# Local attention on one core: where x1 is kept, two buffers for the score image, softmax sums on 32x32 blocks, and five value products a head on GpSimd

## What is computed

```python
x = x + _L0_conv_ref(_gn(x), ...)   # window attention, 16 heads of 16, windows of 49 pixels
x = x + _L1_conv_ref(_gn(x), w_out, b_out)

def _L1_conv_ref(x, w_out, b_out):          # KSIZE 5, PAD 2, NHEADS 8
    patches = extract_patches(x)            # the 25 shifts of each pixel, zeros outside
    p = patches.reshape(N, NHEADS, hdim, K2, H, W)
    q = x.reshape(N, NHEADS, hdim, 1, H, W)
    scores = (p * q).sum(axis=2, keepdims=True)
    att = jax.nn.softmax(scores, axis=3)
    out = (p * att).sum(axis=3).reshape(N, D, H, W)
    out = jnp.einsum('ndhw,od->nohw', out, w_out) + b_out[None, :, None, None]
    return out
```

## Time and profile before

| | |
|---|---|
| median of 3 runs | 1961.32 us (1961.11 to 1963.88) |
| the profiled execution | 1962.19 us |
| its span, first to last instruction | 1960.4 us |
| VectorE / TensorE / GpSimd / ScalarE busy | 83% / 79% / 59% / 53% of the span |
| 16 DMA engines, hardware queue | 20.5% |
| granted TensorE clock | 0.897 |

### The profile page before, as it was taken

The page is one execution under the profiler, slowest core; times in us unless marked ns, Lnnn a source line. Parts: engine busy times, 40 slices in busy tenths (PEclk is TensorE's granted clock), DMA queues, the critical chain, the costliest instruction groups (busy, mean ns, idle before and its releaser), DMA issues.

```text
span 1960.4 us, 53519 instructions
## 1 busy us (share of the span) xinstructions
PE 1557.5 (79%) x21545; PEld 789.1 (40%) x21545; DVE 1627.2 (83%) x2105; ACT 1044.7 (53%) x1927; POOL 1162.3 (59%) x843
## 2 busy tenths in 40 slices
PE   5889999999999999244986949859598595994935
PEld 3667777777777777100221212212122121221413
DVE  5987777777777777479999999899999999999724
ACT  3566677766777666234455554554645545444200
POOL 4434544444545445004869969698796987964800
PEclk9999999999999999675997969969799697996968
DMA  6000000000000000422014140141401404005069
GB/s 266 1 1 33 4 29 33 0 33 0 33 0 33 0 41 14 115 52 52 2 45 112 29 114 16 43 113 28 111 20 43 113 25 113 21 14 223 23 231 401
DMA packets 46596, 126.42 MB, mean 64 GB/s; under 512 B 12644, under 2 KB 24932, under 8 KB 41316
## 3 DMA queue, kind: packets, MB, share of 16 engines
q1 hardware_dynamic: 46436, 124.04, 20.5%
HBM read 79.04 MB, written 38.54 MB: 60 GB/s over the span
## 4 chain that ended last, share of the span: by engine, by line
PE 51%; DVE 28%; issue 10%; ACT 5%; SPq 2%; DMA 1%; DVEq 1%; POOLq 0%; POOL 0%; ACTq 0%
PE PS L1380 11%; PE PS L1267 8%; DVE PS L1140 7%; PE PS L1357 7%; DVE arena L1159 6%; PE PS L1255 6%; PE PS L1343 5%; PE PS L1221 4%; PE PS L1246 3%; DVE consts L1101 3%; DVE arena L1148 2%; PE PS L1400 2%; DVE arena L1053 2%; DVE arena L1134 2%; PE PS L1225 2%
## 5 line engine op out<-in xcount | busy, mean ns | idle before, releaser
L777 POOL TENSOR_TENSOR arena<-arena 128x1856 f32<-128x1856 f32 (+8 forms) x182 | 670.8, 3726 | 237.5 <-ACT arena L911 188.5
L1159 DVE TENSOR_TENSOR arena<-arena,PS 128x1568 f32<-128x1568 f32 x382 | 658.9, 1781 | 26.8 <-PE PS L1380 25.2
L1343 PE MATMUL PS<-arena,consts 128*32 128x285 f32 (+10 forms) x2176 | 252.6, 540 | 197.8 <-POOL arena L777 128.0
L1380 PE MATMUL PS<-arena,consts 32*32 32x392 f32 x12800 | 385.3, 511 | 22.8 <-DVE arena L1159 22.3
L735 POOL TENSOR_TENSOR arena<-arena,consts 128x196 f32<-128x196 f32 x512 | 294.2, 609 | 161.5 <-ACT arena L825 157.0
L953 ACT ACTIVATE PS<-arena 128x392 f32<-128x392 f32 x382 | 190.9, 501 | 344.2 <-DVE arena L1159 342.3
L1267 PE MATMUL PS<-arena 128*128 128x96 f32 x2048 | 265.7, 273 | 3.1 <-ACT arena L838 1.6
L1267 PEld LDWEIGHTS PS<-arena 128*128 128x128 f32 x2048 | 249.9, 192 | 5.3 <-issue 3.5
L1357 PE MATMUL PS<-arena,consts 128*128 128x392 f32 x400 | 193.2, 578 | 52.2 <-DVE arena L1148 52.2
L742 POOL TENSOR_TENSOR arena<-arena 128x392 f32 (+1 forms) x64 | 78.6, 1228 | 255.2 <-DVE arena L1080 255.2
L1343 PEld LDWEIGHTS PS<-arena,consts 128*32 128x32 f32 x2176 | 50.3, 115 | 396.0 <-issue 182.2
(11 more groups left out here) (97 smaller groups left out, 1663.1 us busy)
## 6 DMA issues: line engine op xcount, KB each, us to landing
arena<-x_dram SPq DMA_DIRECT2D x32, 616.0 KB, 7.5
arena<-x_dram SPq DMA_DIRECT2D x240, 77.0 KB, 2.0
arena<-in_x_dram SPq DMA_DIRECT2D x8, 1568.0 KB, 14.7
x_dram<-arena SPq DMA_DIRECT2D x8, 1568.0 KB, 5.2
attn_dram<-arena SPq DMA_DIRECT2D x256, 49.0 KB, 1.9
arena<-x_dram SPq DMA_DIRECT2D x8, 1568.0 KB, 17.6
arena<-attn_dram SPq DMA_DIRECT2D x8, 1568.0 KB, 17.6
out_dram<-arena SPq DMA_DIRECT2D x8, 1568.0 KB, 24.7
```

Of the source, the lines that this page charges most:

```text
L777: nc.gpsimd.tensor_tensor(tile, x_part, by, ALU.mult).then_inc(pool_tile, 1)
L1159: nc.vector.tensor_tensor(by_channel(v_tiles[n % V_RING]), shifted_values(half, k), over_channels(PS[:, 2 + n % W_BANKS, 0:PIX]), ALU.mult ...
L1343: mm = nc.tensor.matmul(PS[g * GROUP:(g + 1) * GROUP, 0, 0:(hi - lo) * cols], fold, tile[:, (g * rows + lo) * cols:(g * rows + hi) * cols] ...
L1380: mm = nc.tensor.matmul(PS[dst, 4 + i, 0:PIX], ident[src, src], tile[src, c * PIX:(c + 1) * PIX], start=done == 0, stop=done == NK - 1)
```

## The change

1. x1 is stored twice: as before (`x1_dram`, unpadded, for the end) and in `x1_wide_dram`, rows of 60 with two zero columns at either side and two zero rows around each channel's images. 12 DMAs of zeros fill it at the start (a new tile `zeros`, 2250 elements a partition); then each unit's 7 rows a partition are stored by one DMA of its own (`widen_x1`, 64 DMAs of 128 x 7 pieces of 56 elements).
2. Strips are loaded with their padding straight into the image (one DMA for a group, source 4 x 32 x 660 elements, destination 128 x 660) and normalised in place; `raw` is gone, and so are the GpSimd memsets of the padding. The score image of x has two buffers for each half, so head j+2 is loaded when head j's products are done. Of heads 0 and 1 the strips of groups 0 and 2 are loaded before the last three pairs are finished.
3. Score products cover only the 56 columns (1568, 1792 or 2016 elements), begin with dy = 2, and have their operands exchanged at dx = -1. No segments any more; the mirror is copied without its outermost columns, which `clear_borders` zeroes with four small copies a head.
4. The sums over the shifts use four 32x32 blocks instead of one 128x128 matrix.
5. In heads 0 to 6 GpSimd takes five value products (16 and 18 of half 0; 17, 21 and 22 of half 1); operands exchanged at dx = -1 there too. In head 7 it takes 17 of 50. The reciprocal comes nine value products before a head's end.
6. A half is stored in 4 DMAs (source 128 x 392, destination 4 x 32 x 392) instead of 16.

```diff
-HALF_PLANE = [(0, 0), (0, 1), (0, 2)] + [(dy, dx) for dy in (1, 2) for dx in range(-2, 3)]
+HALF_PLANE = [(dy, dx) for dy in (2, 1) for dx in range(-2, 3)] + [(0, 2), (0, 1), (0, 0)]
...
-RECIPROCAL_AT = 47
+RECIPROCAL_AT = 9
...
-SHARE_AT = [9, 17]
-POOL_SHARE = [[range(0), range(0)]] * (LH - 1) + [[range(16, NK), range(16, NK)]]
+SHARE_AT = [[9, 13], [18, 21, 24]]
+POOL_SHARE = [[(16, 18), (17, 21, 22)]] * (LH - 1) + [[range(18, NK), range(15, NK)]]
...
-        raw = [room(CH * RAW) for _ in range(2)]
-        xs_halves = room(2 * GROUPS * HALO).rearrange("p (a g h w) -> p a g h w", a=2, g=GROUPS, h=HR)
+        xs_halves = [room(GROUPS * HALO).rearrange("p (g h w) -> p g h w", g=GROUPS, h=HR) for _ in range(4)]
...
+            r0, rows = R - dy, GR + dy
+            X = xs_halves[s_buf(j, a)]
+            tile = ring[RING_AT[step] % S_RING][:, 0:GROUPS * rows * W]
+            here, there = X[:, :, r0:r0 + rows, R:R + W], X[:, :, R:R + rows, R + dx:R + dx + W]
+            if dx == -1:
+                here, there = there, here
...
+            def widen_x1(u):
+                sp.wait_ge(added, u + 1)
+                bp, row = u // NI, u % NI
+                src = xs[:, bp, :].rearrange("p (a i w) -> p a i w", i=NI, w=W)[:, :, row]
+                dst = x1_wide[:, bp].rearrange("p (a i) w -> p a i w", i=NI)[:, :, row, R:R + W]
+                sp.dma_start(dst, src).then_inc(x1_widened[bp > BP // 2], 16)
+
+            def load_for_scores(j, a, g, loaded):
+
+                off = (g // 2 * C + j * HD + a * CH) * LINE + BP // 2 * (g % 2) * H * ROW
+                at = x1_flat[0:1, off:off + 1]
+                src = bass.AP(at.tensor, at.offset, [[LINE, CH], [STRIP, GROUP], [1, HALO]])
+                n = s_buf(j, a)
+                sp.dma_start(xs_halves[n][:, g].rearrange("p h w -> p (h w)"), src).then_inc(loaded[n], 16)
...
+                    dst = attn_dram[b2, j * HD + half * CH:j * HD + half * CH + CH].rearrange("c bp rg n -> c (bp rg) n")
+                    sp.dma_start(dst[:, first:first + GROUP], o_loc[half][:, i]).then_inc(o_stored[half], 16)
...
-                mm = nc.tensor.matmul(lsum, ident, sc[j % 2][:, k, :], start=k == 0, stop=k == NK - 1)
-                if k == NK - 1:
+                for k in range(m * KS, (m + 1) * KS):
+                    for i in range(GROUPS):
+                        rows = slice(i * GROUP, (i + 1) * GROUP)
+                        mm = nc.tensor.matmul(lsum[rows], ident[rows, rows], sc[j % 2][rows, k, :],
+                                              start=k == 0, stop=k == NK - 1)
```

More of the change, by code:

```diff
@@ L222, in merge_orders @@
+        for t in range(S_TILES):
             rows, cols = shape_of(t)
-            lo, hi = segments(rows, cols)[s]
-            last = s == len(segments(rows, cols)) - 1
-            before = ("copy", j, u - 1) if u else ("copy", j - 1, S_UNITS - 1) if j else None
+            before = ("copy", j, t - 1) if t else ("copy", j - 1, S_TILES - 1) if j else None
             for a in range(2):
-                made = ("score", j, t, a)
-                here = ("sum", made) if last else ("part", made)
-                n = RING_AT[made]
-                earlier = ("sum", RING_ORDER[n - 1]) if n and not (a == 1 and not last) else None
-                if last and a == 0:
-                    earlier = ("part", ("score", j, t, 1)) if s else earlier
-                if a == 1 and not last:
-                    earlier = ("part", ("score", j, t, 0))
-                add("pe", here, 0.3 + 1.67e-3 * (hi - lo) * cols, [made, before, earlier], 1.0 if j else 0.1)
@@ L236, in merge_orders @@
-            ends = ("sum", ("score", j, t, 1)) if last else ("part", ("score", j, t, 1))
-            copies = 1 if t == 0 else 2
-            add("act", ("copy", j, u), copies * (0.2 + 0.83e-3 * min(PIX, (hi - lo) * W)),
-                [ends] + ([("weight", n) for n, v in enumerate(V_ORDER) if v[1] == j - 2][-1:] if j >= 2 else [])
-                + ([("total", j - 2, NK - 1)] if j >= 2 else [("pixels", "v", 0, 1, GROUPS + 1)])
-                + ([s for s in RING_ORDER if s[:2] == ("value", j - 2)][-1:] if j >= 2 else []), 0.6 if j else 0.1)
+                n = RING_AT[("score", j, t, a)]
@@ L242, in merge_orders @@
+                add("pe", ("sum", ("score", j, t, a)), 0.2 + 1.67e-3 * rows * cols,
+                    [("score", j, t, a), before, ("sum", RING_ORDER[n - 1]) if n else None], SUM_LAG if j else 0.1)
+            add("act", ("copy", j, t), (1 if HALF_PLANE[t] == (0, 0) else 2) * 0.5,
+                [("sum", ("score", j, t, 1)), ("borders", j)], 0.4 if j else 0.1)
     for j in range(LH):
@@ L281, in merge_orders @@
         orders[eng].append(step)
-    sync = [(end[("pixels",) + LOADS[free_raw(n)] + (GROUPS - 1,)], ("load", n)) for n in range(SLOTS_AT_FIRST, len(LOADS))]
+    sync = []
+    for kind, j, a in LATER:
+        free = [("score", j - 2, S_TILES - 1, a)] if kind == "s" else [s for s in V_ORDER + RING_ORDER if s[:3] == ("value", j - 1, a)]
+        sync.append((max(end[s] for s in free), ("load", kind, j, a)))
     sync += [(end[("reciprocal", j)], ("spread", j)) for j in range(LH)]
@@ L646, in reload_early @@
                     await_half_made(sp, LH - 2, half)
-                for slot in range(2):
-                    sp.wait_ge(scaled[slot], RAW_SLOT.count(slot))
                 for bp in range(early_pairs):
@@ L718, in _ @@
                 nc.gpsimd.memset(v_ch[u], 0.0)
+            nc.gpsimd.memset(zeros, 0.0).then_inc(zeros_ready, 1)
             for q in probs:
```

371 lines of the change are left out of this document (175 added, 196 removed).

## The result

The changed kernel takes 2043.5 us (median of 4 runs, 2043.2 to 2047.9) against 1961.4 of the kernel before beside it: 1.042 times as long, 95% interval 1.040 to 1.044. The forecast was 1901, its range 1860 to 1938. The kernel became slower by the mechanism of the third rival (strips that come too late in ScalarE's queue), and lost more than that rival gave for engines as fast as these were.

What follows compares the result with a forecast made beforehand. VectorE bounds the heads now, GpSimd after the change. Last maximum at 1715, plus 112 to the attention read and 72 to the end, gives 1899; 1.8 more for the execution makes 1901 us, range 1860 to 1938.

Steps and rivals of the forecast that it cites:

- third rival: Head rounds: strips too late in ScalarE's queue, GpSimd stalls 23 us in six rounds, total 2040 us; 8%.
- Work terms: Busy time a head: GpSimd 113.8 us, VectorE 108.7; 72.2 us for reading back, projection and storing at the end.
- second rival: GpSimd's products at dx = -1: exchanging operands does nothing, 3.9 us a round dearer, total 1926 us; 10%.
- Four engines: New score loads: 4 in front at source, 128 at destination, so four DMA engines at 25 GB/s each.
- first rival: DMAs: all 16 engines carry the loads, round 115.2 us, stores end with their issue, total 1867 us; 14%.
- T + 25.5 and T + 29: Each round: arrival of last second-half score strips and of second value half, in us after GpSimd ends a head's scores.
- GpSimd loses about 1.4: Each round: second score copy at T + 34, GpSimd has 34.5 us of work ahead, so loses about 1.4 us.
- VectorE absorbs this: Each round: first exponential at T + 35, needed 28.8 us after the maximum begins; VectorE would otherwise wait for GpSimd.
- Sums over shifts ... at worst they take as long as now: TensorE's 32x32 block sums, costed at nothing: busy 97 of 123 us a head and waited for little.
- What the early start gives, the order of ScalarE takes back: Transition to the heads: VectorE makes only five products early; first maximum at 905 us against 901.4, +4.
- The last head: After the last maximum: VectorE 91 us, GpSimd 83, reciprocal at +76, attention read at +112 (before +126).
- fourth rival: Widening stores: small pieces back up, at 250 ns each the second block starts 118 us later, total 2020; 3%.

Runs made afterwards that it cites:

- e11: On e8, operands no longer exchanged at dx = -1, on either product: 1917.8 us.
- e1: On the changed kernel, each score load cut into its four channels so that all 16 DMA engines share it: 1959.7 us.
- e3: On the changed kernel, score loads and stores both cut into four channels for 16 engines: 1951.8 us.
- e4: On the changed kernel, only the planner's release-to-strips times changed, from 15 us to 16 and 34, 16 and 38; four engines kept: 1967.4 us.
- e14: On the changed kernel, only the softmax sum changed, to 25 steps of one map: 2030.8 us.
- e7: On e6, each map summed by one 128x128 product instead of four 32x32 blocks: 1951.6 us.
- e9: On the changed kernel, four engines kept, with the strip times of e4 and the softmax sum in 25 steps of one map: 1923.6 us.
- e6: On e3, softmax sum in 25 steps of one map instead of 5 of five maps, each counted 0.72 us: 1926.7 us.
- e15: On e13, head 0's score copies no longer behind all strips in ScalarE's order: 1880.6 us.
- e13: On e10, the planner's strip times of e9 (16 and 34, 16 and 38 us): 1903.6 us.
- e10: On e8, last value strips ahead of the x1 reloads in SP's queue, reloads behind the stores of head 6: 1909.3 us.
- e18: On e15, softmax sums no longer put last among TensorE's ready steps, in the last head alone: 1870.2 us.
- e17: On e15, four value products a head on GpSimd instead of five, spreads sorted 8 us earlier into SyncE's queue: 1891.3 us.
- e8: On e6, planner's release-to-strips times of 11 and 17 us for score halves, 11 and 20 for value halves: 1916.8 us.

## Why the prediction was wrong

The gap is 142 us: 8.6 to the first maximum, 11.4 in the first round, 101.7 in the next six, 21 from the last maximum to the attention read, and -0.7 after it.

- **Work terms: right.** VectorE 108.5 (108.7), GpSimd 112.5 (113.8), last stage 71.5 (72.2). The exchange brings 3.95 us a round on GpSimd (3.9), the second rival's price; but undone it costs no time (e11), so that rival's 1926 assumed a bound that is not there.
- **Four engines: right.** 91 GB/s at a share of 0.24, as four times. The Trainium skill's rule on the divisor ("DMA: Bandwidth & Descriptors", why a DMA increments its semaphore by 16) gives the same four. The first rival (16 engines) is out for this kernel.
- **"T + 25.5 and T + 29": wrong by 7.7 and 9.5 us.** I counted the bytes of the eight loads at 25 GB/s an engine, and nothing beside them. Their start was right (T - 1.0, T - 1.5 in the sum), and so was their speed alone (103 GB/s). But for 8 us the value loads behind them share the four engines at 10.9 GB/s each: 0.35 MB instead of 0.82, which costs 4.6 us (an estimate from the three stretches above); some 2.5 more go to the start and the landing. e1, which changed only how the score loads are cut, took 84 us off; e3, with the stores cut too, 92.
- **"GpSimd loses about 1.4", "VectorE absorbs this": the step that failed.** The margin was as thin as the sum said (copy at T + 34 against 34.5 of work ahead), so 8 us later meant 10.4 of stall at once and 16.3 on VectorE, and further stalls of 11 us on GpSimd after it. A round became 17.7 us longer than forecast for 8 us of lateness. That this goes through ScalarE's order is shown by e4, where the strips are as late and only the order differs: 76 us less. The third rival has this mechanism; I made it depend on engines at 18 GB/s or less. Over the whole 34.2 us the four gave 79 GB/s, 19.8 each, so the threshold was missed by little, but the loss was larger than the 10 us a round given for it. Why the stalls after the first one cost so much was not taken apart; the lumps alone are not it, since e14 without them keeps rounds of 133.
- **"Sums over shifts ... at worst they take as long as now": wrong.** The blocks take less (e7), but the change also put five maps into one step where the kernel before had one, which this sentence passed over: in five lumps they block the value sums. Repaired, the rounds go from 122 to 114 (e4 to e9). I had read TensorE's share of busy time as cover; the earlier trace rows's 27.8 us of GpSimd's waits for it were the hint, and I kept 1.4 of 7.0 a round. By map alone 6.8 remain (e6), with the later strips as well 1.7 (e9): 1.4 was right only for an order with both repairs.
- **"What the early start gives, the order of ScalarE takes back": right as a mechanism**, 31.9 us of VectorE's stand, +12 against the kernel before where +4 was said; 3.5 of these 12 are the later end of the first block. e15 shows it: on e13, with the loads on 16 engines, another order takes the first maximum 23 us forward.
- **The last head: +21.** I left out that the last value strips queue behind 9.6 MB of reloads (7.5 us in e10), and that the reciprocal waits for the softmax sums (10.4 us in e18, on e15).
- **The small pieces: cheap.** The late loads wait for the last widening, issued at 801.97, and begin at 806.00; 4.0 us where I counted 6.8. A piece of 224 bytes took 16 ns (median), not 99. My sign for the fourth rival did come, an addition that ends later than 800 (801.94), but it was a poor sign: 3.3 of the 3.5 us are there by 129 us and do not grow, as they would if pieces piled up, and in e1 to e18, which have the same first block, that addition ends anywhere from 797.7 to 803.5. The fourth rival is out.

Still open: why the second round is 120.7 us in e13 and 120.2 in e9, 6 more than the later ones (it is 116.0 in e17), whether four value products would be better than five, and how much of the change's loss in the first round is the transition's. None of these was taken apart.

## What to carry to other kernels

A fixed order made by a planner is only as good as its arrival times and step costs: when a transfer's engines, queue or size change, read in the trace when it lands and put that into the planner, since a late operand in an in-order queue holds up the steps behind it that do not need it. Count into a transfer's time what runs on the same engines meanwhile, also what is issued after it. Count what is behind a wait by its margin: a stage that is covered by 0.5 us is not covered. And keep long steps of an engine that serves two others shorter than the buffers ahead of it, before asking whether their total has become smaller.

## What the runs showed that I had not expected

- Four 32x32 products on the diagonal cost about 0.25 us less than one 128x128 product of the same 392 columns where they stand among other 32x32 products (e6, e7), though TensorE's busy time in both is near full.
- Eight loads on four engines hold SP's queue for 16.2 us while being issued. Cut in four for all engines, the same bytes in 32 loads take 15.7 us (the same place of e1, from 1258.03 on), so four times the DMAs cost SP no time.
- GpSimd can be busy for 99.4% (e11) or for 96.0% (e8) of the same 584.3 us, in which both make some five rounds: an engine near full is not yet the bound.
